# A four-layer kernel on one core: a quarter of the diagonal keys copied by GpSimd, loads and products put in another order, and two products given banks of their own

## The chip, the cores and the metric

The kernel runs on one core of one Trainium2 chip. The metric is the time of one execution in microseconds of the device; the numbers given are medians over runs on the same chip. The engines are called TensorE (PE in the rows), VectorE (DVE), ScalarE (ACT), GpSimd (POOL) and SyncE (SP); "ACTq" and "SPq" are the queues on which an engine issues transfers.

## The reference

The input x is (2, 2048, 512) in fp32. Four layers follow each other, each with a residual. B is the batch, N the tokens, F = 512 the features, H = 16 heads of D = 32.

```python
def modulated_linear(x, s, aff_w, aff_b, w, b):
    style = s @ aff_w.T + aff_b
    w_mod = w[None] * style[:, None, :]
    demod = rsqrt(sum(w_mod * w_mod, axis=2) + EPS)
    return einsum('bni,boi->bno', x, w_mod * demod[:, :, None]) + b

# layer 0: heads attend to each other within one token
kx = modulated_linear(x, s, k_...).reshape(B, N, H, D)
A = softmax(einsum('bnhd,bnjd->bnhj', kx, kx) / sqrt(D))
x = x + modulated_linear(einsum('bnhj,bnjd->bnhd', A, kx).reshape(B, N, F), s, o_...)
# layer 1: a weight of rank 30 for each batch, from a decoder
U = (mu @ W_dec + b_dec).reshape(B, 513, 30)
x = x + x @ (U @ V)[:, :-1] + (U @ V)[:, -1]
# layer 2: modulated linear, clipped
x = x + clip(einsum('blc,oc->blo', x * styles, weight) * dcoefs + bias)
# layer 3: several layer norms of x with gathered gains, three small MLPs,
# six weighted blocks concatenated, then W_int1, silu, W_int2, layer norm
h = ln(ln(x, pw_g[path], pw_b[path]), cp_g[comp], cp_b[comp]); t = ln(x, tm_g[..]); s = ln(x, ms_g[..])
x = x + mlp_ln(concat(w0*h, w1*t, w2*(x+m), w3*(x+n), w4*(x+r), w5*s), ...)
```

## The kernel before

The 4096 tokens are 32 tiles of 128 rows (T = 32), in groups of G = 4 tiles; the 512 features are C = 4 chunks of 128. A product that needs fp32 precision is made of three passes, from a high and a low part of either side (`x_hi`, `x_lo`, `w_high`, `w_low`). The order of work is written out by hand for every engine (`order`, `run_order`), each engine walks it by itself, and semaphores hold them together; so an instruction that waits holds up all that stands behind it on its engine.

**Layer 0** is the loop `attend(s)` for s = -1 to T+7, pipelined over the steps: step s works on several tiles at once. TensorE runs in each step: the transposes of v of tile s-2 (L686) and its scores (L693), the mix of tile s-3 with its weights (L650), the key projection of tile s (L676, 12 products of 512 columns), from s = 8 on the output projection of tile s-8 (L616, 12 products, into the bank `ps_o`), the mask of tile s-1 (L715), then the transposes of the mixed values `om` of tile s-3 (L738). The heads' products are small (32 x 32 blocks), and one operand is laid out as a block diagonal, 128 x 16 x 4 x 32: `k_diag` from the turned keys `kt`, and `at_diag` from the turned weights `at`. ScalarE writes both with four copies of 32 partitions each (`diagonal`, L1076). In a step the chain of a tile is: keys `kb` (VectorE L1427, GpSimd adds the bias, L1849), turned to `kt` (VectorE L1444), `k_diag` (ScalarE), scores, maximum and difference (L1392, L1396), exponential `e` (ScalarE L1103), its sum and inverse (L1416), the division (GpSimd L1843), turned to `at` (L1435), `at_diag` (ScalarE), mix (L650), turned back to `om` (L1403), scaled (GpSimd L1839), L738. GpSimd also scales the input `x_in` by the style (L1832), from which ScalarE and VectorE make the high and low parts for L676, and adds the output bias to the residual (L1826).

From tile 8 on (`SEED_AT`) the mask isn't a product: ScalarE writes it into the score bank beforehand (L1106). `prepare(s)` puts the side work in the steps: the small MLPs in 0 to 7 (their second results turned by `turn_rows(mlp_h2)`, L766, in step 6), the decoder's products L725 in the odd steps 5 to 19, the weights of layers 1 and 2 from step 20 on (`u_t`, the sum of the decoded U and its bias, at L1584 in step 22).

At the start SyncE issues the loads for the styles first (`cond`, `aff_k_t`, `aff_kbt`), then the first input; ScalarE's queue issues the four parts of W_k. TensorE runs six pieces of filling products (`keep_busy`) until the styles' loads have landed, then L89.

**Layers 1 to 3** are the loop `refine(s)`, with the layer-1 and layer-2 work a group of four tiles ahead: `lift(g)` makes `fh` and `fl` of the group's residual stream, `low_rank(g)` L940, `chunk(g, n)` the product of layer 2 (L616 into `ps_y`, evicted as `y` at L1226), and for each tile the layer-3 products: `x_product` (into `ps_3`, which takes the place of `ps_o`), then with t, s and h, silu to `g_out` (L1258), `turn_g`, the last product. GpSimd makes the gathered norms (`xn`, `h`, `tt`, `ss`: L1909 to L1933) and issues the gathers. The last steps of layer 0 overlap with the first of layer 1 (`order` above all from s = T+1 on). W_out's low part, `split("out")` on VectorE (L1631), is made in tile 0 of layer 3.

## Time and profile before

| | |
|---|---|
| runs (three) | 1000.88, 1000.90, 1002.64 us; median 1000.9 |
| the profiled execution | 1001.27 us, span 999.5 us |
| TensorE busy | 972.3 us of the span (97%) |
| GpSimd, VectorE, ScalarE busy | 693.6, 664.3, 501.4 us (69, 66, 50%) |
| the chain that ended last, by engine | PE 70%, POOL 9%, issue 8%, DVE 5%, DMA 3%, ACT 3% |

The span is cut into 40 slices of 25 us in the page; each digit is a busy share in tenths, for the TensorE clock it is what was granted, for DMA the mean busy share of the 16 DMA engines:

```
PE   8989999999999899999999999999999999999995
POOL 5656667575775449787777777778768768777861
PEclk8999999999999999999999999999999999999998
DMA  9644664464422562343133243332332233122220
```

Times are to be read from the start of the span. A row of a timeline gives start, duration, engine, line, operation, output and inputs with shape, and in brackets how long the engine was idle ahead of it and what ended that.

### The profile page before, as it was taken

What the parts mean: (1) busy time and instruction counts of PE and PEld (TensorE: products, weight loads), DVE (VectorE), ACT (ScalarE), POOL (GpSimd) and SP (SyncE); (2) the same over time, 40 slices, a digit from 0 to 9 for tenths busy, and PEclk for the clock granted to TensorE, in tenths of its full rate; (3) what the DMA queues carried; (4) which work ended last, traced back from release to release, by engine and by line L of the source; (5) the groups of instructions that cost most, each with busy time, mean ns of one, the idle gap of its engine ahead of it and who ended that gap; (6) DMA issues with size and microseconds to landing.
All of it is one profiled execution on the core that took longest, in us unless ns stands there. A gap on an engine that the chain in (4) does not pass through costs nothing.

```text
span 999.5 us, 18149 instructions
## 1 busy us (share of the span) xinstructions
PE 972.3 (97%) x6540; PEld 775.5 (78%) x6540; DVE 664.3 (66%) x1215; ACT 501.4 (50%) x792; POOL 693.6 (69%) x634
## 2 busy tenths in 40 slices
PE   8989999999999899999999999999999999999995
PEld 5667777777787677888888888888888888888884
DVE  6688767688878778666665658566567556664542
ACT  2888878787887544343342443334234324323332
POOL 5656667575775449787777777778768768777861
PEclk8999999999999999999999999999999999999998
DMA  9644664464422562343133243332332233122220
GB/s 291 223 144 126 218 225 150 161 218 139 152 90 81 185 213 87 109 121 119 66 109 106 93 130 100 118 110 66 101 116 90 80 101 126 67 91 108 79 76 23
DMA packets 58558, 125.11 MB, mean 125 GB/s; under 512 B 8052, under 2 KB 12534, under 8 KB 57445
## 3 DMA queue, kind: packets, MB, share of 16 engines
q1 hardware_dynamic: 46116, 80.95, 24.2%
q0 software_dynamic: 11776, 41.95, 13.4%
q8 instruction: 53, 0.87, 0.3%
q10 hardware_dynamic: 576, 1.05, 0.3%
q14 instruction: 37, 0.30, 0.1%
HBM read 105.98 MB, written 17.95 MB: 124 GB/s over the span
## 4 chain that ended last, share of the span: by engine, by line
PE 70%; POOL 9%; issue 8%; DVE 5%; DMA 3%; ACT 3%; SPq 1%; POOLq 0%; DVEq 0%; ACTq 0%
PE ps L609 34%; PE ps_k L676 7%; PE ps_y L616 6%; PE ps_o L616 5%; PE tp L621 4%; PE ps_v L650 2%; PE ps_s L693 2%; DMA xb<-in_x_wide 1%; PE ps_u L725 1%; PE ps_z L940 1%; POOL h L1909 1%; PE tp L952 1%; DMA id_rows<-in_id_rows 1%; PE ps_vt L686 1%; PE ps_t L738 1%
## 5 line engine op out<-in xcount | busy, mean ns | idle before, releaser
L1895 POOL TENSOR_TENSOR rstd<-var_eps,half 128x1 f32<-128x1 f32 x95 | 53.6, 565 | 101.5 <-DVE var_eps L1649 100.7
L1258 ACT ACTIVATE g_out<-ps 128x512 f32<-128x512 f32 x32 | 19.1, 597 | 167.2 <-PE ps L1057 167.2
L1839 POOL TENSOR_TENSOR om<-om,bc 128x512 f32<-128x512 f32 x32 | 41.4, 1292 | 65.1 <-DVE om L1403 65.0
L1076 ACT ACTIVATE at_diag<-at 32x512 f32<-32x512 f32 x128 | 80.3, 628 | 9.2 <-DVE at L1435 7.6
L1655 DVE TENSOR_SCALAR shift_n<-mean_var,rstd 128x1 f32<-128x1 f32 x96 | 20.5, 214 | 96.6 <-POOL rstd L1895 94.2
L1076 ACT ACTIVATE k_diag<-kt 32x512 f32<-32x512 f32 x128 | 80.2, 626 | 1.1
L1826 POOL TENSOR_SCALAR xb<-xb,bias_o 128x512 f32<-128x512 f32 x32 | 52.9, 1653 | 39.9 <-DMA xb<-in_x_wide 39.8
L1212 ACT ACTIVATE h<-h,shift_n,rstd 128x512 f32<-128x512 f32 x32 | 26.1, 816 | 84.7 <-DVE shift_n L1655 84.7
L1635 DVE TENSOR_TENSOR t_lo<-tp,t_hi 128x512 fp32r<-128x512 f32 x64 | 43.8, 684 | 29.8 <-ACT t_hi L1208 29.8
L676 PE MATMUL ps_k<-wk_hi,xh 128*128 128x512 f32 x128 | 54.1, 426 | 0.5 <-DVE xl L1451 0.5
L1955 POOL DMA_INDIRECT path_rows<-in_path,pid x32 | 39.5, 1235 | 19.5 <-POOL pid L1943 19.5
L609 PE MATMUL ps<-wx_high,x_hi 128*128 128x512 f32 x128 | 53.0, 414 | 0.0
L609 PE MATMUL ps<-wt_high,t_hi 128*128 128x512 f32 x128 | 52.7, 412 | 0.0
L616 PE MATMUL ps_o<-oh,wo_hi 128*128 128x512 f32 x128 | 50.3, 393 | 0.5 <-DVE xb L1383 0.5
L1928 POOL TENSOR_TENSOR o<-f,x3s 128x512 f32<-128x512 f32 x31 | 50.4, 1625 | 0.6 <-DMA out<-o 0.4
L609 PE MATMUL ps<-wx_high,x_lo 128*128 128x512 f32 x128 | 50.4, 393 | 0.0
L1917 POOL TENSOR_TENSOR tt<-xn,comp_rows 128x512 f32<-128x512 f32 x32 | 50.2, 1569 | 0.0
L609 PE MATMUL ps<-wt_high,t_lo 128*128 128x512 f32 x128 | 50.1, 392 | 0.0
L609 PE MATMUL ps<-wt_low,t_hi 128*128 128x512 f32 x128 | 50.0, 391 | 0.0
L609 PE MATMUL ps<-wx_low,x_hi 128*128 128x512 f32 x128 | 50.0, 390 | 0.0
L616 PE MATMUL ps_o<-ol,wo_hi 128*128 128x512 f32 x128 | 50.0, 390 | 0.0
L676 PE MATMUL ps_k<-wk_lo,xh 128*128 128x512 f32 x128 | 49.9, 394 | 0.0
(317 smaller groups left out, 3193.9 us busy)
## 6 DMA issues: line engine op xcount, KB each, us to landing
raw<-in_dec_w SPq DMA_DIRECT2D x30, 512.0 KB, 5.8
...
```

What stands on the lines that cost most here:

```text
L609: mm = nc.tensor.matmul(out_ps[:, :], x[:, c, :], w_[:, c, :], start=first and n == 0, stop=last and n == len(terms) - 1)
L616: mm = nc.tensor.matmul(out_ps[:, :], w_[:, c, at_], x[:, c], start=n == 0, stop=n == len(terms) - 1)
L621: mm = nc.tensor.transpose(bank[:, c, :], src[:, c * P:(c + 1) * P], ident[:, :])
L676: mm = nc.tensor.matmul(ps_k[:, :], x[:, c, :], w_[:, c, :], start=first and n == 0, stop=last and n == len(some) - 1)
L1076: last = nc.scalar.activation(dst[g, :, q, :], src[g, :, :], ACT.Copy)
L1635: nc.vector.tensor_tensor(lo[n][:, :, :], bank[:, :, :], hi[n][:, :, :].bitcast(F32), ALU.subtract).then_inc(lo_ready[n], 1)
L1826: nc.gpsimd.tensor_scalar(xb[n % 3][:, :], xb[n % 3][:, :], bias_o[:, fo:fo + 1], None, ALU.add).then_inc(xb_ready, 1)
L1839: nc.gpsimd.tensor_tensor(om[:, :], om[:, :], bc[:, STYLE_O, t // TB, :], ALU.mult).then_inc(mix_step, 1)
L1895: nc.gpsimd.tensor_tensor(rstd[:, k:k + 1], var_eps[:, k:k + 1], half[:, :], ALU.pow).then_inc(norm_step[k], 1)
L1917: nc.gpsimd.tensor_tensor(tt[:, :], xn[:, :], comp[:, F:2 * F], ALU.mult).then_inc(t_ready, 1)
L1928: nc.gpsimd.tensor_tensor(o[:, :], f2[:, :], x3s[f % 4][:, :], ALU.add).then_inc(o_ready, 1)
L1955: nc.gpsimd.indirect_dma_start(dst[:, :], None, I[table], bass.IndirectOffsetOnAxis(pid[:, k:k + 1], 0)).then_inc(landed, 16)
```

## The change

- **Start.** The loads of `cond` and `aff_kbt` go from SyncE's queue to the head of ScalarE's, ahead of W_k; `keep_busy` runs four pieces in place of six.
- **Diagonal keys.** In the steps 2 to 8 (`SHARED`) ScalarE copies three quarters of `k_diag`; GpSimd copies the fourth (`last_quarter`), as the first instruction of its step, ahead of `x_in`'s scaling. TensorE's scores wait for it through `xm_ready`, whose values `x_count` counts on.
- **Mask.** The last tile's mask is a product again (`seeded`).
- **`lift(0)`** on ScalarE (1 instruction, `fh`) goes from ahead of step T+1 to within it, behind `e` and `w_high`, ahead of `at_diag`.
- **Banks.** The output product of tile 31 goes to `ps_t`'s bank (`o_bank`) and waits for `ol` of the last tile in place of the residual of tile 30; `x_product(0)`, which writes where `ps_o` was, now waits for the residual of tile 31 (`x1_ready`, T). The fourth chunk's product of layer 2 goes to `tp[1]` (`y_bank`) and waits for the last mix alone; the first turn of `tt` then waits for that chunk's eviction.
- **W_out's low part** goes on VectorE from tile 0 to tile 1, ahead of that tile's `g_lo` and `s_lo`, with the ends of layers 1 and 2 behind these. Tile 0's silu is kept in a buffer of `x3s` (`g_rows`), so that it waits for stores of layer 0 and not for that.
- **Small ones.** `u_t`'s sum goes from VectorE to GpSimd (step 22); `turn_rows(mlp_h2)` goes from step 6 to step 7.

The core of the diff:

```diff
     for s in range(-1, T + 1):
         yield "attend", s
-    if engine == "ACT":
-        yield "lift", 0
     yield "attend", T + 1
...
+    SHARED = range(2, 9)
...
+        def seeded(t):
+            return SEED_AT <= t < T - 1
+        def g_rows(d):
+            return x3s[3][:, :] if d == 0 else g_out[:, :]
+        def x_count(t):
+            return t + 1 + len([s for s in SHARED if s < t])
...
+        def o_bank(n):
+            return ps_o[:, :] if n < T - 1 else ps_t[:, :, :].rearrange("p c q -> p (c q)")
+        def y_bank(n):
+            return tp[1][:, :, :].rearrange("p c q -> p (c q)") if n == C - 1 else ps_y[:, :]
...
@@ SyncE
-            sp.dma_start(cond[:, :, :], I["cond_t"].rearrange("(c p) b -> p c b", p=P)).then_inc(style_k_in, 16)
-            sp.dma_start(aff_kbt[:, :, :], I["aff_bt"]).then_inc(style_k_in, 16)
@@ TensorE
-            keep_busy(ps_o, 6)
+            keep_busy(ps_o, 4)
...
                 pe.wait_ge(ol_ready, G * (g + 1))
-                if later(n, 1):
+                if n == T - 1:
+                    pe.wait_ge(ol_ready, T)
+                elif later(n, 1):
                     pe.wait_ge(x1_ready, n)
...
                     pe.wait_ge(k_diag_ready, t + 1)
-                    if t >= SEED_AT:
+                    if t + 1 in SHARED:
+                        pe.wait_ge(xm_ready, x_count(t + 1) + 1)
+                    if seeded(t):
...
-                if has(1) and s - 1 < SEED_AT:
+                if has(1) and not seeded(s - 1):
...
-                if s == 6:
+                if s == 7:
                     pe.wait_ge(mlp_step, 14)
                     pe.wait_ge(table_ready, 3)
                     turn_rows(mlp_h2, ps_rows_t).then_inc(rows_turned, 1)
-                if s == 7:
...
-                if later(n, 1):
+                if n == C - 1:
+                    pe.wait_ge(v_ready, T)
+                elif later(n, 1):
                     pe.wait_ge(y_ready, n)
...
                     pe.wait_ge(w_lo_ready, 1)
-                    pe.wait_ge(ol_ready, T)
+                    pe.wait_ge(x1_ready, T)
                 product(ps_3, "x3", Wt["x"], last=False).then_inc(l3x_done, 1)
...
-                        pe.wait_ge(v_ready, T)
+                        pe.wait_ge(y_ready, C)
                     turn(tt, tp[1]).then_inc(turned["t"], 1)
@@ ScalarE
+            act.dma_start(cond[:, :, :], I["cond_t"].rearrange("(c p) b -> p c b", p=P)).then_inc(style_k_in, 16)
+            act.dma_start(aff_kbt[:, :, :], I["aff_bt"]).then_inc(style_k_in, 16)
...
-            def diagonal(dst, src):
-                for q in range(Q):
+            def diagonal(dst, src, count=Q):
+                for q in range(count):
...
-                    if SEED_AT <= t + 1 < T:
+                    if seeded(t + 1):
...
-                    diagonal(k_diag[p], kt[p]).then_inc(k_diag_ready, 1)
+                    diagonal(k_diag[p], kt[p], Q - 1 if s in SHARED else Q).then_inc(k_diag_ready, 1)
...
+                if s == T + 1:
+                    lift(0)
@@ VectorE
                 if s == 22:
-                    dve.wait_ge(u_back, 16 * B)
-                    nc.vector.tensor_tensor(u_t[:, :], u_got[0:B * LOW, :], tab_part[0:B * LOW, :], ALU.add).then_inc(u_step, 1)
...
+                if b == 3:
+                    dve.wait_ge(turned["g"], 1)
...
-                if ahead and k >= 1:
+                if c == 1:
+                    split("out")
+                elif ahead and k >= 1:
                     if s != 0:
                         layer1_end(g, k - 1)
                     layer2_end(g, k - 1)
...
                     low("s", c, tp[1])
+                if c == 1:
+                    layer1_end(g, k - 1)
+                    layer2_end(g, k - 1)
                 if c == 0:
                     split("h")
                     low("h", 0, tp[0])
                     hot(0)
-                    split("out")
                     x3_low(1)
@@ GpSimd
+            def last_quarter(s):
+                t, p, last = s - 1, (s + 1) % 2, slice(D * (Q - 1), D * Q)
...
+                pool.wait_ge(k_step, nth(KEYS, "turned", t + 1))
+                if later(t, 2):
+                    pool.wait_ge(scores_done, t - 1)
...
+                nc.gpsimd.tensor_copy(k_diag[p][last, :, Q - 1, :], kt[p][last, :, :]).then_inc(xm_ready, 1)
+                pool.wait_ge(xm_ready, x_count(s) + 1)
             def attend(s, has):
+                if s in SHARED:
+                    last_quarter(s)
...
+                if s == 22:
+                    pool.wait_ge(u_back, 16 * B)
+                    nc.gpsimd.tensor_tensor(u_t[:, :], u_got[0:B * LOW, :], tab_part[0:B * LOW, :], ALU.add).then_inc(u_step, 1)
```

GpSimd in the steps 2 and 3 of layer 0 (`wo_sq` and `mlp_rstd` are side work), before:

```order
L1860 TENSOR_TENSOR wo_sq<-wo_raw 128x512 x2
L1832 TENSOR_TENSOR x_in<-x_in,style_t 128x512
L1843 TENSOR_TENSOR e<-e,rinv 128x512
L1849 TENSOR_TENSOR kb<-kb,bias_k 128x512
L1860 TENSOR_TENSOR wo_sq<-wo_raw 128x512 x2
L1863 TENSOR_TENSOR mlp_rstd<-mlp_var,half 96x1
L1832 TENSOR_TENSOR x_in<-x_in,style_t 128x512
L1839 TENSOR_TENSOR om<-om,bc 128x512
L1843 TENSOR_TENSOR e<-e,rinv 128x512
L1849 TENSOR_TENSOR kb<-kb,bias_k 128x512
```

and with the change:

```order
L1914 TENSOR_TENSOR wo_sq<-wo_raw 128x512 x2
L1870 COPY k_diag<-kt 32x16x32
L1886 TENSOR_TENSOR x_in<-x_in,style_t 128x512
L1897 TENSOR_TENSOR e<-e,rinv 128x512
L1903 TENSOR_TENSOR kb<-kb,bias_k 128x512
L1914 TENSOR_TENSOR wo_sq<-wo_raw 128x512 x2
L1917 TENSOR_TENSOR mlp_rstd<-mlp_var,half 96x1
L1870 COPY k_diag<-kt 32x16x32
L1886 TENSOR_TENSOR x_in<-x_in,style_t 128x512
L1893 TENSOR_TENSOR om<-om,bc 128x512
L1897 TENSOR_TENSOR e<-e,rinv 128x512
L1903 TENSOR_TENSOR kb<-kb,bias_k 128x512
```

One copy (L1870) stands at the head of each of the two steps, ahead of `x_in` and all that follows on this engine.

ScalarE in the last steps of layer 0, from `e` of tile 30 on, before (`a_buf` is a piece of layer 2's weight, `fh` the high part of the residual stream for layers 1 and 2):

```order
L1106 ACTIVATE ps_s<-mask_rows 128x512
L1076 ACTIVATE k_diag<-kt 32x16x32 x4
L1124 ACTIVATE w_high<-a_buf 128x512
L1076 ACTIVATE at_diag<-at 32x16x32 x4
L1235 ACTIVATE fh<-xt 128x2048
L1087 ACTIVATE oh<-ps_t 128x4x128
L1097 ACTIVATE v<-ps_vt 128x512
L1103 ACTIVATE e<-low 128x512
L1124 ACTIVATE w_high<-a_buf 128x512
L1076 ACTIVATE at_diag<-at 32x16x32 x4
```

and with the change:

```order
L1100 ACTIVATE k_diag<-kt 32x16x32 x4
L1148 ACTIVATE w_high<-a_buf 128x512
L1100 ACTIVATE at_diag<-at 32x16x32 x4
L1111 ACTIVATE oh<-ps_t 128x4x128
L1121 ACTIVATE v<-ps_vt 128x512
L1127 ACTIVATE e<-low 128x512
L1148 ACTIVATE w_high<-a_buf 128x512
L1261 ACTIVATE fh<-xt 128x2048
L1100 ACTIVATE at_diag<-at 32x16x32 x4
```

The mask's copy into `ps_s` is gone, and `fh` stands four instructions further back, straight ahead of the last `at_diag` (tile 31's), behind `e` and `w_high`.

VectorE at the end of tile 0 of layer 3 and in tile 1, before (`h`, `tp` are the norm's inputs, the suffixes `_lo` the low parts for the products):

```order
L1721 TENSOR_SCALAR one_hot<-id_rows,codes 128x128
L1631 TENSOR_TENSOR wout_low<-out_raw,wout_high 128x2048
L1697 TENSOR_TENSOR x_lo<-xt,x_hi 128x512
L1641 BN_STATS stats<-h 128x6
L1645 BN_AGGR mean_var<-stats 128x2
L1649 TENSOR_SCALAR var_eps<-mean_var 128x1
L1655 TENSOR_SCALAR shift_n<-mean_var,rstd 128x1
L1641 BN_STATS stats<-tp 128x6
L1645 BN_AGGR mean_var<-stats 128x2
L1649 TENSOR_SCALAR var_eps<-mean_var 128x1
```

and with the change:

```order
L1671 BN_AGGR mean_var<-stats 128x2
L1675 TENSOR_SCALAR var_eps<-mean_var 128x1
L1681 TENSOR_SCALAR shift_n<-mean_var,rstd 128x1
L1667 BN_STATS stats<-tp 128x6
L1671 BN_AGGR mean_var<-stats 128x2
L1675 TENSOR_SCALAR var_eps<-mean_var 128x1
L1661 TENSOR_TENSOR t_lo<-tp,t_hi 128x512
L1742 TENSOR_TENSOR x3s<-tp,shift 128x512
L1681 TENSOR_SCALAR shift_n<-mean_var,rstd 128x1
L1657 TENSOR_TENSOR wout_low<-out_raw,wout_high 128x2048
L1661 TENSOR_TENSOR g_lo<-tp,g_hi 128x512
L1661 TENSOR_TENSOR s_lo<-tp,s_hi 128x512
```

The piece begins two rows later, behind `x_lo`'s and the statistics' first rows. `wout_low` stands ten rows further back than before, behind a shift of tile 1, with `g_lo` and `s_lo` behind it.

## Rows read from the trace of the kernel before

**Rows 1.** Waits of PE: engine, line, waited for, total us, times, longest us
```profile
PE ps_v L650 <- ACT at_diag L1076: 4.3, 5, 1.9
...
PE ps_t L738 <- DVE ol L1373: 1.2, 2, 0.7
...
PE tp L621 <- issue: 0.9, 1, 0.9
...
PE tp L621 <- POOL tt L1917: 0.9, 1, 0.9
...
PE ps_y L616 <- ACT y L1226: 0.6, 1, 0.6
...
PE ps_o L616 <- DVE xb L1383: 0.5, 1, 0.5
```

**Rows 2.** Engine time by stretch: busy us (count) per engine, PEclk, DMA share, GB/s
```profile
76.00:77.00 1.00, 1.00 (x6) 1.00 (x7) 1.00 (x2) 0.98 (x2) 0.00 (x0) 0.52 0.00 0
...
88.87:246.00 157.13, 156.17 (x1653) 116.97 (x1657) 119.37 (x193) 126.98 (x214) 106.05 (x84) 1.00 0.51 176
...
400.60:999.50 598.90, 587.37 (x2881) 489.08 (x2879) 355.49 (x711) 209.66 (x323) 437.95 (x420) 1.00 0.30 96
```

**Rows 3.** Timeline, start: start us, duration us, engine line operation [idle before <-releaser]
```profile
7.22 3.09 PE L89 MATMUL ps_x<-cond,wsq 128*128 128x2 f32 x16 [1.63 <-DMA aff_kbt<-in_aff_bt]
...
34.29 1.04 POOL L1832 TENSOR_TENSOR x_in<-x_in,style_t 128x512 f32<-128x512 f32 x1 [2.92 <-DMA x_in<-in_x_turned]
...
35.98 1.05 POOL L1843 TENSOR_TENSOR e<-e,rinv 128x512 f32<-128x512 f32 x1 [0.65 <-DVE rinv L1416]
```

**Rows 4.** Timeline, three durations that bound the GpSimd copy's price
```profile
0.87 0.53 POOL L1813 MEMSET mask_rr<- 128x512 f32 x1
...
71.52 2.54 ACT L1076 ACTIVATE k_diag<-kt 32x512 f32<-32x512 f32 x4
...
360.58 3.37 POOL L1826 TENSOR_SCALAR xb<-xb,bias_o 128x512 f32<-128x512 f32 x1 [5.84 <-DMA xb<-in_x_wide]
```

**Rows 5.** Timeline, steps 3 and 4
```profile
45.20 1.30 POOL L1839 TENSOR_TENSOR om<-om,bc 128x512 f32<-128x512 f32 x1 [0.40 <-DVE om L1403]
...
58.88 1.90 PE L650 MATMUL ps_v<-at_diag,v 128*32 128x128 f32 x32 [1.86 <-ACT at_diag L1076]
```

**Rows 6.** Timeline, steps 6 to 8
```profile
74.73 2.55 ACT L1076 ACTIVATE at_diag<-at 32x512 f32<-32x512 f32 x4
...
75.99 0.88 PE L766 MATMUL ps_o<-ident,xb 96*128 96x96 f32 x4 [2.01 <-DVE xb L1497]
...
77.65 1.94 PE L693 MATMUL ps_s<-k_diag,kt 128*32 128x128 f32 x32
...
77.88 1.66 POOL L1870 TENSOR_TENSOR demod_t<-vareps_ko,half_ko 128x8 f32<-128x8 f32 x1 [2.50 <-DVE vareps_ko L1549]
...
81.78 1.29 POOL L1839 TENSOR_TENSOR om<-om,bc 128x512 f32<-128x512 f32 x1 [1.22 <-DVE om L1403]
...
88.80 0.50 PE L676 MATMUL ps_k<-wk_hi,xh 128*128 128x512 f32 x1
```

**Rows 7.** Timeline, step 22 and the steps of the last tiles
```profile
237.02 0.68 DVE L1584 TENSOR_TENSOR u_t<-u_got,tab_part 64x512 f32<-64x512 f32 x1
...
331.53 1.91 ACT L1235 ACTIVATE fh<-xt 128x2048 fp32r<-128x2048 f32 x1
...
331.91 0.69 DVE L1396 TENSOR_TENSOR low<-ps_s,mx 128x512 f32<-128x512 f32 x1
...
373.82 0.74 DVE L1383 SCALAR_TENSOR_TENSOR xb<-ps_o,demod_t,xb 128x512 f32<-128x512 f32 x1
...
373.98 0.48 PE L609 MATMUL ps<-wx_high,x_hi 128*128 128x512 f32 x1
```

**Rows 8.** Timeline, layers 1 to 3, tiles 0 and 1
```profile
390.25 2.28 DVE L1631 TENSOR_TENSOR wout_low<-out_raw,wout_high 128x2048 fp32r<-128x2048 f32 x1
...
390.32 3.35 POOL L1911 TENSOR_TENSOR h<-h,path_rows 128x512 f32<-128x512 f32 x1
```

32 lines of the change are left out of this document (23 added, 9 removed).

## The prediction

> **What bounds the kernel now.** I read the busy times first: TensorE is busy 972.3 of 999.5 us, so all that any rearrangement can win is its 27.2 us of idle time and what it runs at a lowered clock. The engine time by stretch says where that is [rows 2]: from 88.9 to 246 us TensorE is busy 156.17 of 157.13, at full clock, and from 400.6 us to the end 587.37 of 598.90. In these two stretches it is the bound; a microsecond won ahead of one is carried to the end, and one lost as well. The waits of TensorE then name the places outside them: 4.3 us for the block-diagonal weights in five waits, 1.2 for `ol`, in tile 1 of layer 3 two of 0.9 [rows 1], 1.6 for the first loads [rows 3], and 2.0 for a small sum ahead of L766 [rows 6]. The change has an edit near each of these. So I follow three stretches: start to 88.8, the end of layer 0 to 374, and tiles 0 and 1 of layer 3 up to 400.
>
> **Start (loads, `keep_busy`).** L89 starts at 7.22, having waited 1.63 for `aff_kbt`, the third issue of SyncE's queue [rows 3]. At the head of another queue it lands earlier and two filling pieces fewer are in the way: 1.6 to 2.0 us earlier for the first styles and the first `x_in`. I count nothing of it at the end, because the next thing that is late is a transfer: the fourth tile's input is waited for by GpSimd until 34.29, after 2.92 us of idleness, and the bytes ahead of it are the same. Behind it GpSimd waits 0.65 more for the inverse sum [rows 3], which comes from the compute chain; at most that is won. Bounds: 0 and 0.65 us at step 2.
>
> **The fourth quarter on GpSimd (steps 2 to 8).** It saves ScalarE one of four copies, 2.54 / 4 = 0.63 us a step, and costs GpSimd one of 32 x 512. No row of before shows it. The nearest are GpSimd's 128 x 512 memset, 0.53, and its slowest one-input pass of that size, 3.37 [rows 4]. An ordinary pass with two inputs of that size, `e`, takes 1.05 [rows 3]. The copy reads one operand, so I put it between memset and `e` at 0.75, and keep 0.53 and 3.37 for the range.
> In step 3 the copy, then `x_in`, stand ahead of `om`, which had 0.40 of idle time [rows 5]: 0.75 - 0.40 = 0.35 late for `om`, `e` and `kb`, against 0.63 saved ahead of ScalarE's `at_diag`: TensorE's mix comes some 0.2 earlier. In step 4 the wait before the mix is 1.86 [rows 5], and its chain is `kb`, `at`, `at_diag`, in which `k_diag` has no part: `at_diag` starts when `at` is done, so that wait stays.
>
> **Steps 6 and 7 (`turn_rows` a step later, and the copy).** The wait of 2.01 ahead of L766 goes [rows 6]. In the microsecond behind it the granted clock is 0.52 [rows 2], the lower level of 1.2 GHz after TensorE had stood idle, and the 32 score products take 1.94 us [rows 6]. So there seems to be 2.0 plus about 1.3 of slowed products to win. Most of it isn't there: the mix of that step needs `at_diag`, which ScalarE ends at 74.73 + 2.55 = 77.28 [rows 6], so TensorE now waits there, and then GpSimd binds. From the end of `demod_t` (77.88 + 1.66 = 79.54) it had `x_in` 1.05, idle 1.22 waiting for `om`, `om` 1.29, `e` 1.05 [rows 6], then `kb`. With the change: 0.2 earlier, copy 0.75, and no idle: 0.2 + 1.22 - 0.75 = 0.67 earlier for `kb`, and so for the keys of step 8, which TensorE starts at 88.80 [rows 6] and from which on it is full. **I take 0.6 for all that lies ahead of 88.8**; with the clock lowered again at the new wait it is 0.3.
>
> **Step 22 (`u_t` on GpSimd).** VectorE spends 0.68 on it [rows 7], ahead of the maximum from which `ol` follows, for which TensorE waits 0.6 to 0.7 (one of two such waits [rows 1]). GpSimd idles at that point. Bounds 0 and 0.68; **0.4**, since the next operation that is late, `at_diag`, is not helped in full.
>
> **End of layer 0 (mask, `lift(0)`).** ScalarE's mask copy and `fh`, 1.91 us up to 333.44, stood ahead of two evictions and the `e` of tile 31, which started at 334.3. The difference it needs is ready at 331.91 + 0.69 = 332.60 [rows 7], so `e` starts some 1.6 earlier; of that GpSimd's and VectorE's order lets 1.05 through to `at` and `at_diag`. `fh` now stands ahead of `at_diag`, and fits in before `at` is done. Against three of TensorE's waits for `at_diag` and `ol` in this stretch: **1.0** at 344 us, bounds 0.5 and 1.6.
>
> **Banks.** They take away the waits for `y` (0.6) and for the residual (0.5) [rows 1]. But `x_product(0)` starts at 373.98 and from now on waits for the residual of tile 31, which VectorE made from 373.82 to 374.56, behind other work [rows 7]. TensorE arrives earlier, and waits there instead: **0** for TensorE, and 0.5 to 0.6 earlier for VectorE and GpSimd; bounds -0.6 and 1.1.
>
> **W_out's low part.** It takes 2.28 us of VectorE in tile 0, and a GpSimd pass that overlaps it takes 3.35 [rows 8] where one of the same shape takes 1.30 [rows 5]. `tt` comes 0.9 late from that, and 0.9 more is waited behind it [rows 1]. In tile 1 it stands ahead of `g_lo` and `s_lo`, which TensorE needs a group of 12 products later, and beside it GpSimd issues gathers. The two waits of 0.9 go, and some 0.2 come back: **1.6**, bounds 0.2 and 2.1.
> The Trainium skill ("SBUF — State Buffer", section "SBUF: two separate sides") says that VectorE and GpSimd share a port pair as an exclusive lock: a VectorE instruction with two SBUF inputs and a GpSimd instruction that reads SBUF block each other for their whole length. By that rule the 3.35 above is a pass that stood still, so trace and rule agree; but it also speaks against the copies: the fourth rival.
>
> **Sum.** 0.6 + 0.4 + 1.0 + 0 + 1.6 = 3.6 us. The profiled execution took 1001.27 us, its span 999.5; it becomes 997.7. The median of the runs is 0.4 lower than that execution, 1000.9, so I forecast **997.3 us**.
>
> **Rivals.**
> *The clock stays up early.* If TensorE's shorter idle times in the steps 5 to 7 don't bring the clock down, the products that ran at 0.52 [rows 2] take half the time, the chains that begin at them move too, and up to 2.6 us are won ahead of 88.8 in place of 0.6: 995.3. For it: the longest of the waits go or shrink. Against: GpSimd's order in step 7, as worked out.
> *The wait moves with W_out's part.* The 2.28 us [rows 8] now hold up `g_lo` and `s_lo`, TensorE waits for these in tile 1, and the late 1.6 is given back: 998.9. For it: nothing on VectorE got shorter. Against: the new place has 12 products of slack.
> *GpSimd becomes the bound, slower.* At the place where the copy stands ahead of `x_in`, `om`, `e` and `kb`, it must fit in 0.40 (step 3) and 1.22 (step 7) of slack, with the 0.6 that the early part wins: 2.2 us for two copies. At the contended price of 3.37 each [rows 4] they cost 6.74, so 4.5 are lost early, against 3.0 won late: 1.5 slower, 1002.4. It decides the sign from a copy of (2.2 + 3.0) / 2 = 2.6 us. Against it: only a GpSimd pass that ran beside one of VectorE's took that long.
> *The copies stand behind `xl`.* VectorE's `xl`, two inputs, follows straight on the `kt` that releases the copy. If the copy waits it out, it comes 0.68 later, the length of such a VectorE pass [rows 7], in both steps in which it counts, 3 and 7: 1.4 us worse, 998.7. For it: the pass of 3.35 beside `wout_low` [rows 8], the case that the Trainium skill's rule describes. Against it: the copy and `xl` are released at nearly the same moment, and step 7's copy stands behind `demod_t`, after `xl`.
> *The start gains nothing and the early edits don't meet the wait*: some 1000.0.
>
> **How the numbers follow.** About 2.0 us (0.2%) is what a measurement of this kernel can tell from no change: faster means under 998.9, slower over 1002.9. Main case 0.40, of which 0.39 lies under 998.9 and 0.01 within. Clock 0.22, faster. Moved wait 0.18, at the boundary: 0.09 faster, 0.09 same. Copies behind `xl` 0.10: 0.06 faster, 0.04 same. GpSimd bound 0.05: 0.01 same, 0.04 slower. The last 0.05: 0.04 same, 0.01 slower. Together faster 0.76, same 0.19, slower 0.05. The range: below, the clock case's 2.6 with the upper bounds 0.6, 1.6 and 2.1 of the others are 6.9, so 994.0, and I go to 993.8; above, the lower bounds 0, 0.5 and 0.2 with the early 0.6 lost in part leave 0.5: 1000.4.
>
> **What would show it.** Right: L89 near 5.5 us; the copies at 0.6 to 1.1 us; no wait ahead of L766 but one of 1.5 to 2 ahead of the mix in step 7; TensorE's key projection of step 8 at 88.2; no wait for `y` nor for the residual of tile 30, but one for that of tile 31; `h`'s pass at 1.3 in tile 1. Wrong: copies over 2 us, the wait in step 4 longer than 1.9, TensorE waiting for `g_lo` or `s_lo`, or a key projection of step 8 before 87 us.

## The result, and the profile after

| | before | with the change |
|---|---|---|
| median of 20 runs | 999.36 us (996.49 to 1002.84) | 1003.79 us (1000.2 to 1006.9, without one disturbed execution) |
| ratio, 95% interval | | 1.0037 [1.0027, 1.0048] |
| profiled execution, span | 1001.27, 999.5 us | 1003.55, 1001.8 us |
| TensorE busy | 972.3 us | 973.0 us |
| GpSimd, ScalarE busy | 693.6, 501.4 us | 702.1, 497.9 us |

The forecast was 997.3 us, 3.6 less than before, in a range of 993.8 to 1000.4. The kernel became 0.37% slower by the ratio, 3.7 us (the two medians lie 4.4 apart). TensorE does the same work and idles 28.8 us in place of 27.2; some of its work also ran at the lower rate.

Its waits with the change, in the view of [rows 1]:

```profile
PE ps_v L667 <- ACT at_diag L1100: 6.2, 6, 1.9
...
PE tp L638 <- DVE t_lo L1661: 3.5, 3, 2.9
...
PE ps_t L759 <- DVE ol L1402: 1.6, 2, 1.2
...
PE ps L626 <- DVE xb L1412: 1.5, 1, 1.5
...
PE ps_x L654 <- DVE wk_sq L1395: 0.7, 1, 0.7
...
PE ps_t L759 <- POOL om L1893: 0.8, 2, 0.5
```

The wait for the block-diagonal weights has grown from 4.3 to 6.2 us, and three waits are new: 2.9 for `t_lo` in one place, 1.5 for a residual, 0.7 for W_k's squares. The two waits of 0.9 in tile 1, that for `y`, that for the residual of tile 30 and that ahead of `turn_rows` are gone, as forecast. So nearly every wait that the change aimed at has gone, and others stand in their place.

To see where, one can lay marks on TensorE's timeline and take the time between two of them. This also keeps apart what varies from one execution to the next: single executions of the kernel before lie 6 us apart, and much of the spread that the traces show arises ahead of the first mark. The marks are the first products on `u_row` in step 2, the mixes (L650) of tiles 6, 20, 21 and 31, `x_product(0)`, and the products with the table (`one_hot`) that close tiles 0, 1 and 2 of layer 3. From the timelines, in us; "before, again" is a second execution of the kernel before (run b2), told of below:

```
                              before   before, again   the change
span start to u_row            35.05          34.84        37.14
u_row to mix of tile 6         61.44          59.86        59.76
mix of tile 20 to 21           11.23          11.24        11.81
mix of tile 21 to 31           94.58          94.54        93.72
mix of 31 to x_product(0)      33.53          33.52        33.64
table product 0 to 1           18.82          18.79        16.77
table product 1 to 2           22.04          22.02        26.49
```

**Start.** The styles' products begin earlier, as meant, and what follows is late. With the change:

```profile
5.76 3.57 PE L89 MATMUL ps_x<-cond,wsq 128*128 128x2 f32 x16 [0.80 <-DMA aff_kbt<-in_aff_bt]
...
11.98 1.93 PE L654 MATMUL ps_x<-wk_sq,sq_wide 128*32 128x512 f32 x8 [0.73 <-DVE wk_sq L1395]
...
17.43 1.91 PE L695 MATMUL ps_k<-wk_lo,xh 128*128 128x512 f32 x4
...
10.62 0.63 ACT L1086 ACTIVATE wk_hi<-wk_raw 128x512 fp32r<-128x512 f32 x1 [0.78 <-DMA wk_raw<-in_w_k_t]
```

and before:

```profile
16.20 1.09 PE L676 MATMUL ps_k<-wk_lo,xh 128*128 128x512 f32 x4
...
8.47 0.63 ACT L1064 ACTIVATE wk_hi<-wk_raw 128x512 fp32r<-128x512 f32 x1 [0.82 <-DMA wk_raw<-in_w_k_t]
```

L89 is 1.46 us earlier (7.22, [rows 3]). But the last of W_k's four parts, now behind two small loads, is ready for ScalarE at 10.62 and not at 8.47. TensorE waits for its squares, and its four products of a first-tile term, 1.09 us before, take 1.91: half the rate. The key projection of step 8, forecast for 88.2, starts at 89.22 (88.80 before).

**Copies.** With the change, GpSimd's copies in the steps 2 and 3 and TensorE's waits ahead of the mixes of tiles 1, 2, 4 and 5:

```profile
33.32 0.96 POOL L1870 COPY k_diag<-kt 32x512 f32<-32x512 f32 x1
...
46.28 0.61 POOL L1870 COPY k_diag<-kt 32x512 f32<-32x512 f32 x1
...
53.66 1.08 PE L667 MATMUL ps_v<-at_diag,v 128*32 128x128 f32 x32 [0.76 <-ACT at_diag L1100]
...
61.71 1.08 PE L667 MATMUL ps_v<-at_diag,v 128*32 128x128 f32 x32 [1.87 <-ACT at_diag L1100]
...
78.56 1.08 PE L667 MATMUL ps_v<-at_diag,v 128*32 128x128 f32 x32 [1.91 <-ACT at_diag L1100]
...
88.21 1.08 PE L667 MATMUL ps_v<-at_diag,v 128*32 128x128 f32 x32 [0.70 <-ACT at_diag L1100]
```

The seven copies take 0.96, 0.61, 0.93, 0.99, 0.93, 0.61 and 0.98 us, all between the ends of 0.53 and 3.37. In the two steps that the sum priced, 3 and 7, it is 0.61, and with the gaps around it the copy makes `x_in` 0.8 later (against the kernel without copies, run ns): that price, 0.75, was right. The other five begin while VectorE's `xl` runs; each of them ends 0.48 us after `xl`, as in step 5:

```profile
61.24 0.64 DVE L1480 TENSOR_TENSOR xl<-x_in,xh 128x512 fp32r<-128x512 f32 x1
...
61.37 0.99 POOL L1870 COPY k_diag<-kt 32x512 f32<-32x512 f32 x1 [1.57 <-DVE kt L1473]
```

That is the mechanism of the fourth rival, but not in the steps 3 and 7, where no `xl` runs beside the copy. What went wrong is in step 3, on ScalarE, before and with the change:

```profile
48.28 2.55 ACT L1076 ACTIVATE at_diag<-at 32x512 f32<-32x512 f32 x4
...
51.05 2.55 ACT L1100 ACTIVATE at_diag<-at 32x512 f32<-32x512 f32 x4 [0.99 <-DVE at L1464]
```

Before, ScalarE came to `at_diag` just as `at` was done. With the change ScalarE is free earlier and waits 0.99 us, because `at` is late by the copy: its relief wins nothing there. The wait of 1.86 in step 4 [rows 5] has stayed; the wait of 2.01 ahead of L766 [rows 6] has become 1.91 ahead of the mix of tile 4; and 0.70 ahead of tile 5's is new.

**Step 22.** `u_t`'s sum on GpSimd, and the wait for `ol`:

```profile
232.49 1.26 POOL L1939 TENSOR_TENSOR u_t<-u_got,tab_part 64x512 f32<-64x512 f32 x1
...
243.09 0.63 PE L759 MATMUL ps_t<-ident,om 128*128 128x128 f32 x4 [1.25 <-DVE ol L1402]
```

It takes 1.26 us there (0.68 on VectorE, [rows 7]), ahead of the residual's bias, which VectorE waits for; the wait of 0.7 [rows 1] has become 1.25.

**Banks.** TensorE's wait ahead of `x_product(0)`, and VectorE's residual of tile 31 that ends it:

```profile
374.28 0.47 PE L626 MATMUL ps<-wx_high,x_hi 128*128 128x512 f32 x1 [1.46 <-DVE xb L1412]
...
373.38 0.75 DVE L1412 SCALAR_TENSOR_TENSOR xb<-ps_t,demod_t,xb 128x512 f32<-128x512 f32 x1
```

The start is 374.28, 373.98 before [rows 7]. (One thing told ahead of the prediction is to be corrected: `ps_3` stands where `ps_t` was, not where `ps_o` was. That is why `x_product(0)` has to wait for tile 31 once its product is in `ps_t`.)

**W_out's low part.** Tiles 0 and 1 of layer 3, and then TensorE in tile 2:

```profile
390.61 1.29 POOL L1968 TENSOR_TENSOR h<-h,path_rows 128x512 f32<-128x512 f32 x1
...
397.34 2.28 DVE L1657 TENSOR_TENSOR wout_low<-out_raw,wout_high 128x2048 fp32r<-128x2048 f32 x1
...
397.60 2.95 POOL L2012 DMA_INDIRECT path_rows<-in_path,pid  x1 [0.28 <-POOL pid L2000]
...
420.20 1.09 PE L638 MATMUL tp<-ident,ss 128*128 128x128 f32 x4 [2.95 <-DVE t_lo L1661]
...
421.08 1.06 PE L638 MATMUL tp<-ident,h 128*128 128x128 f32 x4
```

GpSimd's pass L1968 takes 1.29 and not 3.35 [rows 8]: that step was right, and tile 1 is 2.05 us shorter. But the part, 2.28 us long, now begins 0.26 ahead of the first gather for tile 2. That gather's issue takes 2.95 us and ends at 400.55, 0.93 after the part has ended. GpSimd's norms of tile 2 come late, then `t_lo`; TensorE, ahead by 2, waits 2.95 for it, and its transposes then take 1.09 for the 0.60 that they take elsewhere. The granted clock there:

```profile
420.00:422.00 2.00, 1.80 (x9) 1.83 (x10) 1.65 (x3) 2.00 (x4) 1.92 (x3) 0.50 0.00 0
```

is 0.50, the lower level, 1.2 GHz. Tile 2 loses 4.45 us.

### The profile page after: what moved, and what is told of

It reads as the page before. It is cut to its first block, busy times and chain, and to the rows that moved or that the text cites. A ratio compares the mean times of both kernels' runs of the same rounds, so it can differ in the third digit from the quotient of the medians.

```text
span 1001.8 us, 18164 instructions
## 1 busy us (share of the span) xinstructions
PE 973.0 (97%) x6537; PEld 776.1 (77%) x6537; DVE 664.9 (66%) x1214; ACT 497.9 (50%) x784; POOL 702.1 (70%) x642
## 4 chain that ended last, share of the span: by engine, by line
PE 72%; POOL 10%; issue 7%; DVE 5%; DMA 3%; ACT 2%; SPq 0%; ACTq 0%; POOLq 0%; DVEq 0%
PE ps L626 36%; PE ps_k L695 7%; PE ps_y L633 7%; PE ps_o L633 5%; PE tp L638 5%; PE ps_v L667 2%; PE ps_s L714 2%; DMA xb<-in_x_wide 1%; PE ps_u L746 1%; PE tp L974 1%; PE ps_z L962 1%; PE ps_t L759 1%; POOL h L1966 1%; PE ps_vt L705 1%; POOL om L1893 1%
## 5 line engine op out<-in xcount | busy, mean ns | idle before, releaser
L1100 ACT ACTIVATE k_diag<-kt 32x512 f32<-32x512 f32 x121 | 75.9, 627 | 1.1
L2012 POOL DMA_INDIRECT path_rows<-in_path,pid x32 | 41.8, 1305 | 19.7 <-POOL pid L2000 19.7
L1985 POOL TENSOR_TENSOR o<-f,x3s 128x512 f32<-128x512 f32 x31 | 52.5, 1694 | 0.2
L695 PE MATMUL ps_k<-wk_hi,xl 128*128 128x512 f32 x128 | 50.1, 396 | 0.0
L626 PE MATMUL ps<-ws_high,s_hi 128*128 128x512 f32 x128 | 49.8, 389 | 0.0
```

The lines of the kernel that those rows point to most:

```text
L626: mm = nc.tensor.matmul(out_ps[:, :], x[:, c, :], w_[:, c, :], start=first and n == 0, stop=last and n == len(terms) - 1)
L695: mm = nc.tensor.matmul(ps_k[:, :], x[:, c, :], w_[:, c, :], start=first and n == 0, stop=last and n == len(some) - 1)
L1100: last = nc.scalar.activation(dst[g, :, q, :], src[g, :, :], ACT.Copy)
L1985: nc.gpsimd.tensor_tensor(o[:, :], f2[:, :], x3s[f % 4][:, :], ALU.add).then_inc(o_ready, 1)
L2012: nc.gpsimd.indirect_dma_start(dst[:, :], None, I[table], bass.IndirectOffsetOnAxis(pid[:, k:k + 1], 0)).then_inc(landed, 16)
```

## The experiments

Each run has its median and, behind it, its ratio to the kernel before, measured beside it on the same chip, with a 95% interval. The ratios hold the whole; the marks, from one trace of each run, hold the parts.

### w0: W_out's low part back in tile 0

```diff
-                if c == 1:
-                    split("out")
-                elif ahead and k >= 1:
+                if ahead and k >= 1:
...
                     hot(0)
+                    split("out")
                     x3_low(1)
```

> The changed kernel with W_out's low part back in tile 0 of layer 3, all else as changed. Theory (the wait moved to the gathers): with the part in tile 1 the first gather of tile 2 is issued in 2.95 us instead of 1.05, its results come late, TensorE waits 2.95 us for t_lo in tile 2 and runs its next products at the lower rate, 4.45 us in all, after a gain of 2.04 in tile 1. Undone, the distance from x_product(0) to the table product of tile 2 (62.0 us with the change, 59.6 before) is 59.0 to 60.0, and the time is 2.4 us below the changed kernel's. Rival (the 2.9 us wait is an accident of that one execution): the distance is that of the changed kernel less nothing systematic, and the time rises by the 2.04 of tile 1.

Measured: 1001.74 us, 1.0021 [1.0005, 1.0038], by the ratios 1.6 below the change (2.4 expected; the intervals overlap). The gather, and TensorE's waits:

```profile
400.55 1.05 POOL L2008 DMA_INDIRECT path_rows<-in_path,pid  x1 [0.28 <-POOL pid L1996]
...
PE tp L638 <- DVE t_lo L1661: 1.3, 3, 0.6
...
PE tp L638 <- POOL tt L1970: 0.9, 1, 0.9
...
PE tp L638 <- issue: 0.9, 1, 0.9
```

The gather takes 1.05 again, the two waits of 0.9 are back, the wait for `t_lo` is 0.6. From `x_product(0)` to table product 2: 60.4 us, 62.0 with the change, 59.6 before; 59.0 to 60.0 was expected. The part was in tile 1 in six executions with its own subtraction: the gather took 2.94 or 2.95 in all of them, the stretch from table product 0 to 1 16.8 us in all six, and from 1 to 2 24.0 to 27.9, 26.0 on average. With the part in tile 0, ten other kernels and executions give 18.8 and 22.0 to 22.2, w0 22.8. So the move wins 2.0 and loses 3.9 on average.

The long gather is no accident; what follows from it varies. In two of the six (ns and t6) the granted clock stays at 1.00, and TensorE waits 1.8 and 2.1 us:

```profile
416.38 0.63 PE L638 MATMUL tp<-ident,ss 128*128 128x128 f32 x4 [1.81 <-DVE t_lo L1661]
```

From `x_product(0)` to table product 2 these two take 59.6 and 59.8 us, as before. In the other four the wait is 2.4 to 3.0 us, the granted clock falls to 0.50 behind it, and the stretch takes 61.8 to 63.4. So the gather gives back the 2.0 that were won, and the longer wait with the fallen clock makes the loss. Why the first norm behind the gathers starts up to 1.2 us later in one execution than in another, these runs don't show.

### k6: six filling pieces

```diff
-            keep_busy(ps_o, 4)
+            keep_busy(ps_o, 6)
```

> The changed kernel with six filling pieces at the start in place of four. Theory (clock): with four pieces TensorE stands idle from 4.96 us, and its products then run at the lower rate until 20.5 us (before: until 14); six pieces bring the full rate back by 14 us, the products of the first tile (16.8 to 20.5 us) take 1.8 us less and the first mix starts at 43 us or below in place of 44.79; time 1 to 2 us below the changed kernel's. Rival (order of the loads: W_k's parts come 0.9 us later behind the two small ones, and the squares wait for them): six pieces change nothing or cost 0.5, the first mix stays at 44.8.

Measured: 1003.39 us, 1.0048 [1.003, 1.0066], no better than the change where 1 to 2 us were expected; first mix at 43.63, the full rate by 16. The wait for the squares was 3.5 us. One execution against another said that the pieces help by 1.2 us, the medians that they don't. That was left for the runs below.

### ns: no copies on GpSimd

```diff
-    SHARED = range(2, 9)
+    SHARED = range(0)
```

> The changed kernel with all four quarters of the diagonal keys on ScalarE again. Theory (GpSimd binds): a copy takes 0.96 us and stands ahead of x_in, om, e and kb; the mixes of tiles 1 and 5 start 0.7 and 1.2 us late for it; without it the key projection of step 8 comes 1.0 to 1.5 us earlier against the first mix, and the time is 1 us below the changed kernel's. Rival (ScalarE binds, the copies help): at_diag comes 0.63 later in steps 2 to 8 and the time rises by 0.6 or more.

Measured: 1001.24 us, 1.0017 [1.0004, 1.003]. From u_row to the mix of tile 6: 58.28 us, 59.76 with the change, and no wait ahead of tile 5's mix. The time is 2.0 us below the change's by the ratios. Over the six executions that have all seven copies this stretch takes 59.4 to 61.2 us, 60.3 on average, without the one with the earlier `turn_rows`; over six without any 58.3 to 59.9, 58.7 on average: a difference of 1.6 us.

The time between single mixes says more, for from the mix of tile 1 on it repeats within 0.06 us where the clock doesn't fall. With a copy in step 3 the mixes of tiles 0 and 1 lie 8.5 to 8.9 us apart, without it 8.2 (8.4 in boa4, and 9.0 in two runs that wait for an input). From the mix of tile 3 to that of tile 6 it is 26.4 with the copies of the steps 7 and 8 and 25.6 without. So the copies cost 0.3 to 0.7 in step 3 and 0.8 in step 7, 1.1 to 1.5 us. The rest of the 1.6 is a fallen clock in step 4, which makes the time between the mixes of tiles 2 and 3 10.4 us in place of 8.8. It fell in four of the eight traces with a copy in step 3 (k6, ks, t6, c37) and in one of the ten without (the first of the kernel before): more often with the copy, but too few to decide.

### ud: `u_t` back on VectorE

```diff
+                    nc.vector.tensor_tensor(u_t[:, :], u_got[0:B * LOW, :], tab_part[0:B * LOW, :], ALU.add).then_inc(u_step, 1)
...
-                    nc.gpsimd.tensor_tensor(u_t[:, :], u_got[0:B * LOW, :], tab_part[0:B * LOW, :], ALU.add).then_inc(u_step, 1)
```

> The changed kernel with the sum for u_t back on VectorE. Theory: on GpSimd it takes 1.26 us ahead of the residual's bias, VectorE's residual waits for that, and TensorE's wait for ol in step 22 grew from 0.67 to 1.25; undone it is 0.7 again and the time 0.6 lower. Rival: the wait has another cause (the stretch begins 0.4 later anyway); it stays at 1.2.

Measured: 1003.51 us, 1.0036 [1.0019, 1.0054], which can't tell 0.6 us. The marks can: from the mix of tile 20 to 21 it is 11.21, with the change 11.81. All seven traces with the sum on GpSimd have 11.76 to 11.82, all eleven with it on VectorE 11.19 to 11.25. It costs 0.6.

### ks: the start undone

```diff
+            sp.dma_start(cond[:, :, :], I["cond_t"].rearrange("(c p) b -> p c b", p=P)).then_inc(style_k_in, 16)
             sp.dma_start(affs[0], I["aff_k_t"].rearrange("(c p) f -> p c f", p=P)).then_inc(style_k_in, 16)
+            sp.dma_start(aff_kbt[:, :, :], I["aff_bt"]).then_inc(style_k_in, 16)
...
-            keep_busy(ps_o, 4)
+            keep_busy(ps_o, 6)
...
-            act.dma_start(cond[:, :, :], I["cond_t"].rearrange("(c p) b -> p c b", p=P)).then_inc(style_k_in, 16)
-            act.dma_start(aff_kbt[:, :, :], I["aff_bt"]).then_inc(style_k_in, 16)
```

> The changed kernel with its start undone (cond and aff_kbt on SyncE's queue again, six filling pieces). Theory (W_k's parts behind two small loads): the wait ahead of the products of squares goes from 0.7 to 3.9 us to none or under 0.5, TensorE is at the full rate by 15 us, the first mix starts at 42.5 to 43.5 us instead of 43.5 to 46.2; time 1.5 below the changed kernel's. Rival (the first mix is set by the transfer of the fourth tile's input and by the copy in step 2): it stays above 44.5.

Measured: 1000.82 us, 1.0012 [0.9998, 1.0027]; a wait of 0.2 for the squares, first mix at 41.44, earlier than expected. It is 2.5 us better than the change.

### t6: `turn_rows` in step 6

```diff
-                if s == 7:
+                if s == 6:
                     pe.wait_ge(mlp_step, 14)
                     pe.wait_ge(table_ready, 3)
                     turn_rows(mlp_h2, ps_rows_t).then_inc(rows_turned, 1)
+                if s == 7:
```

> The changed kernel with turn_rows in step 6 again. Theory (a wait there is 2.0 us, but another one takes its place): TensorE waits 1.5 to 2.0 ahead of it and no longer 1.9 ahead of the mix of tile 4; the mix starts 1.0 to 2.0 us later and what is left at the mix of tile 6 is 0.5 to 1.5 later than with the change. Rival (GpSimd's order in step 7 binds alone): the mix of tile 6 comes at the same distance from the first mix, 52.1 us.

Measured: 1002.15 us, 1.0024 [1.0008, 1.0039], and in the trace:

```profile
75.98 0.81 PE L787 MATMUL ps_o<-ident,xb 96*128 96x96 f32 x4 [2.00 <-DVE xb L1527]
```

The wait is there again, 2.00, and that ahead of tile 4's mix is gone. From u_row to the mix of tile 6: 61.81, against 60.3 on average with the later place; but the clock fell in step 4 here, which is 1.6 us. From the mix of tile 3 to that of tile 6 it is 27.20, and 26.39 with the change: the later place wins 0.8 beside the copies. Without copies it wins 1.6 (27.2 in both executions of the kernel before, 25.6 in ns). So the two edits don't add: with the early `turn_rows` the copy in step 7 costs nothing (27.20 with and without it), with the late one 0.8. The ratio doesn't bear the 0.8 out: t6 lies 1.3 us under the change where it should lie above it. The intervals overlap, and that stays open.

### b2: the kernel before, again

> The kernel before once more, unchanged, for its profile: how far the first 40 us vary from one execution to the next. If the first mix starts within 0.5 us of 42.7 the start's 2.1 us of the changed kernel is its own; if it starts over 44 it is chance.

Measured: 999.34 us (one execution), first mix at 42.48, within the 0.5. In the steps up to 8 this execution was 1.6 us faster than the first, since the clock did not fall in step 4. That is as much as several terms of my sum.

### best1: four parts undone

The edits of w0, ns, ud and ks together.

> The changed kernel with four of its parts undone: the loads and the filling pieces as before, no copies on GpSimd, W_out's low part in tile 0, the sum for u_t on VectorE. Left are the later turn_rows, the last tile's mask and lift(0), and the banks. Theory (the kept parts are sound, the four are what cost): to x_product(0) the kernel takes 370.5 to 372.0 us of the span (before 374.0), tiles 0 to 2 as before, time 2 to 3.5 us below the kernel before. Rival (the kept parts win nothing either, the start varies by more than they do): within 1 us of the kernel before.

Measured: 997.14 us, 0.9973 [0.9962, 0.9983]: faster than the kernel before. `x_product(0)` at 370.88, table products as before. The later `turn_rows` and the pair of the last tile's mask and `lift(0)` are sound together; no run takes the mask and `lift(0)` apart. `x_product(0)` still waits 1.5 us for the residual.

### sh, c37: copies in some of the steps

On best1, `SHARED = range(4, 7)` and `SHARED = (3, 7, 8)`.

> The fastest version so far (the changed kernel with the start, the copies, W_out's part and u_t undone) with copies on GpSimd in the steps 4 to 6 alone. Theory (a copy costs only where GpSimd's chain x_in, om, e, kb is the late one, steps 3, 7 and 8): from the products on u_row in step 2 to the mix of tile 6 it stays at 58.3 us, plus or minus 0.3. Rival A (any copy costs its 0.96 us or a part): 59 or more. Rival B (ScalarE's relief helps in step 4, where TensorE waits 1.9 us for at_diag): 57.7 or less.

Measured: 995.58 us, 0.9963 [0.9951, 0.9976]; u_row to the mix of tile 6: 58.28, the same as best1's 58.27.

> The fastest version so far with copies on GpSimd in the steps 3, 7 and 8 alone. Theory: this carries the whole cost of the seven copies, 1.5 to 2.7 us: the same stretch takes 59.7 us or more where no lowered clock hits it, with a wait of 0.75 ahead of the mix of tile 1 and 0.7 ahead of that of tile 5. Rival (the cost is spread over all copies): 58.9 or less.

Measured: 998.34 us, 0.9989 [0.9977, 1.0002]; 61.00 us, and the two waits:

```profile
51.06 1.08 PE L669 MATMUL ps_v<-at_diag,v 128*32 128x128 f32 x32 [0.75 <-ACT at_diag L1100]
...
87.18 1.08 PE L669 MATMUL ps_v<-at_diag,v 128*32 128x128 f32 x32 [0.71 <-ACT at_diag L1100]
```

Part of the 61.0 is a lowered clock in step 4 (0.50 granted from 60 to 62 us), 1.6 us. Without it 59.4 would be left, between the theory's 59.7 and the rival's 58.9, and 1.1 over best1. So the copies in the steps 3, 7 and 8 carry the cost of 1.1 that all seven have at the least; in the steps 4 to 6 they neither cost nor win, though TensorE waits 1.9 us for ScalarE's `at_diag` there. The relief of ScalarE lies ahead of a wait for `at`, as the prediction had it.

### bo: tile 31's product in its old bank

```diff
-            return ps_o[:, :] if n < T - 1 else ps_t[:, :, :].rearrange("p c q -> p (c q)")
+            return ps_o[:, :]
...
-                if n == T - 1:
-                    pe.wait_ge(ol_ready, T)
-                elif later(n, 1):
+                if later(n, 1):
...
-                    pe.wait_ge(x1_ready, T)
+                    pe.wait_ge(ol_ready, T)
```

on best1.

> The fastest version so far with tile 31's output product in its old bank (the fourth chunk of layer 2 keeps its own). Theory (own bank for tile 31 only moves the wait): TensorE waits 0.5 for the residual of tile 30 and no longer 1.5 for that of tile 31; x_product(0) starts 0.5 to 1.0 us earlier against the last mix (33.6 us with the bank) and the time falls by as much. Rival (x_lo is ready no earlier): 33.6 stays within 0.2.

Measured: 995.88 us, 0.9966 [0.9953, 0.9979]. The wait of 1.5 is gone, and in its place:

```profile
PE ps_o L635 <- DVE xb L1410: 0.5, 1, 0.5
```

From the mix of tile 31 to `x_product(0)`: 32.87, and 32.64 to 32.92 in all five executions of this form, 33.4 to 33.7 in the others. Of the two new banks, that of tile 31 cost 0.8 us, and that of the fourth chunk wins about 0.7. The ratios can't tell this: 0.9966 here, 0.9973 for best1 and 0.9963 for sh, which both have the new bank.

### w1: a plain copy in place of W_out's low part

It leaves out the subtraction; the copy has one input.

```diff
+                    if n == "out":
+                        nc.vector.tensor_copy(flat(w_lo), flat(staged_raw[n])).then_inc(w_lo_ready, 1)
```

> The changed kernel with W_out's low part replaced by a plain copy of W_out at the same place of tile 1: the subtraction is left out, so the last product has a wrong low part. Theory (a VectorE pass that reads two operands in the on-chip buffer holds up GpSimd, a gather's issue too): with one operand the first gather of tile 2 is issued in 1.05 us instead of 2.95, GpSimd's norms of tile 2 start 1.9 earlier, TensorE's wait for t_lo in tile 2 falls from 2.95 to about 1. Rival (the gather waits for something else there, or the plain copy holds it up as well): it stays at 2.9.

Measured: 999.59 us, 0.9998 [0.9984, 1.0011]:

```profile
393.69 1.22 DVE L1658 CAST wout_low<-out_raw 128x2048 fp32r<-128x2048 f32 x1
...
393.95 1.88 POOL L2015 DMA_INDIRECT path_rows<-in_path,pid  x1 [0.28 <-POOL pid L2003]
...
414.11 0.63 PE L638 MATMUL tp<-ident,ss 128*128 128x128 f32 x4 [0.49 <-DVE t_lo L1664]
```

The theory was wrong in its reason. The copy, with one operand, takes 1.22 us and holds up the gather just as well: the issue ends at 395.83, 0.92 after the copy, as it ended 0.93 after the subtraction. It is shorter only because VectorE's pass is. The consequence stood: with a gather 1.07 us shorter TensorE waits 0.5 in tile 2, not 2.95, and table product 2 comes 58.2 us after `x_product(0)` in place of 62.0.

The Trainium skill ("SBUF — State Buffer", section "SBUF: two separate sides") tells this of a copy: while VectorE runs an instruction in a 2-port mode, which an fp32 copy triggers, GpSimd is locked out of the shared ports and can't write the descriptors of its transfers. The trace agrees for the copy, 1.22 us: the gather ends 0.92 behind it. For the subtraction, 2.28 us, the trace shows the same, 0.93 behind it.

### bol4, boa6, boa4: queue and filling pieces apart

On bo: four pieces with SyncE's queue; six with ScalarE's; four with ScalarE's.

> The fastest version (bo) with four filling pieces, the loads on SyncE's queue. Theory (the queue is the cause): as bo, the products on u_row at 34.4 us plus or minus 1, the time within 0.8 us of bo's 0.9966 of the kernel before. Rival (the pieces are the cause): u_row at 35.5 or later, TensorE at the lower rate until 20 us, 1 to 2 us slower.

> bo with cond and aff_kbt at the head of ScalarE's queue and six filling pieces. Theory (queue): 1 to 2 us slower than bo, the ratio to the kernel before 0.998, u_row at 35.5 to 37. Rival (pieces): as bo.

> bo with the whole start of the change: the two loads on ScalarE's queue and four pieces. Both theories: 1.5 to 2.5 us slower than bo; if it is within 0.8 us of bo, the start costs nothing and the difference between the changed kernel and the one with its start undone was chance.

| | queue of the two loads | pieces | ratio to before | u_row at |
|---|---|---|---|---|
| bo | SyncE | 6 | 0.9966 [0.9953, 0.9979] | 32.94 |
| bol4 | SyncE | 4 | 0.9979 [0.9968, 0.9991] | 34.62 |
| boa6 | ScalarE | 6 | 0.9997 [0.9983, 1.001] | 35.68 |
| boa4 | ScalarE | 4 | 0.999 [0.9976, 1.0004] | 37.90 |

The queue costs 1.1 us with four pieces, where the intervals overlap, and 3.1 with six, 2.1 on average. The pieces show nothing clear: six are 1.3 better on SyncE's queue (so bol4 isn't within the 0.8 of bo that was expected), 0.7 worse on ScalarE's and 1.1 worse in k6, all with intervals that overlap. In nine traces with the loads on ScalarE's queue its last W_k part comes at 9.89 to 11.54 us, in nine with SyncE's at 7.88 to 8.87; the products on `u_row` at 36.4 and 34.3 on average. boa4 shows what follows, its engine time by stretch:

```profile
10.00:14.00 4.00, 1.73 (x8) 0.23 (x8) 3.35 (x6) 1.38 (x3) 1.57 (x2) 0.50 1.07 267
...
14.00:18.00 4.00, 4.00 (x17) 3.49 (x14) 0.56 (x3) 0.60 (x1) 0.44 (x1) 0.50 1.06 279
...
18.00:20.00 2.00, 2.00 (x6) 1.52 (x6) 1.26 (x5) 0.00 (x0) 2.00 (x3) 0.50 1.08 360
```

```profile
PE ps_x L654 <- DVE wk_sq L1393: 3.2, 1, 3.2
```

and bol4's:

```profile
10.00:14.00 4.00, 4.00 (x14) 1.50 (x13) 3.52 (x6) 1.23 (x2) 1.30 (x1) 0.50 1.07 254
...
14.00:18.00 4.00, 3.87 (x20) 2.98 (x20) 1.16 (x6) 0.00 (x0) 2.16 (x3) 0.92 1.07 324
...
18.00:20.00 2.00, 2.00 (x5) 0.49 (x6) 1.53 (x4) 1.10 (x2) 0.86 (x1) 1.00 1.07 376
```

TensorE is idle for 3.2 us up to 12.27, waiting for W_k's squares, and is granted 0.50 until about 22 us; bol4, busy from 8 on, is at 0.92 from 14 to 18 and at the full clock behind it.

### shbo: sh and bo together

> bo with copies on GpSimd in the steps 4 to 6. If the relief of ScalarE in these steps is worth something the ratio is 0.9955 or less; if the copies there are neutral, as the stretch of 58.3 us in both says, it is bo's 0.9966 within the interval.

Measured: 996.32 us, 0.9971 [0.9961, 0.9981], as bo. The copies in the steps 4 to 6 are worth nothing. Between bo, sh and shbo no ratio decides; bo has the fewest parts and is the version to keep.

## Why the prediction was wrong, point by point

The terms, in us won, as forecast and as the marks give them (averages over the executions named above):

| step | forecast | measured |
|---|---|---|
| start: two loads, filling pieces | 0 | -2.1 |
| copies and `turn_rows`, up to step 8 | +0.6 | +0.3 (-1.3 and +1.6) |
| `u_t` on GpSimd | +0.4 | -0.6 |
| mask and `lift(0)` | +1.0 | +0.9 |
| banks | 0 | -0.1 (+0.7 and -0.8) |
| W_out's low part | +1.6 | -1.9 |
| sum | +3.6 | -3.5 |

For the copies and `turn_rows` the stretch from u_row to the mix of tile 6 is taken without the falls of the clock (1.6 us each where it fell in step 4, 0.7 in w0): 59.6 on average with both edits (59.4 to 59.8), 59.9 before.

- **Start: wrong, by leaving out what the step displaces.** The prediction counted how much earlier the styles come and called the rest hidden behind the fourth tile's input. It never asked what stands behind the two loads on ScalarE's queue: W_k's four parts, and behind the last of them TensorE's squares. They came 2.4 us later on average, more than the two issues, 0.48 and 0.51 us; where the rest comes from the runs don't show. That the fourth tile's input swallows what is won is half true: with the earliest start, bo's, 0.9 us were lost again between the first mix and the second, and there GpSimd waits 4.6 us for that input.
- **Copies: right on GpSimd, wrong for TensorE in step 3.** The price of 0.75 was right (0.8), and so was step 7: from `demod_t` to `kb` it is 5.66 us and 6.34 before, 0.68 earlier for the forecast 0.67. In step 3 the prediction set ScalarE's saving of 0.63 against a delay of 0.35 and had the mix 0.2 earlier. The two don't subtract: `at_diag` starts when the later of ScalarE and `at` is ready, and `at` was late. The mix came 0.3 to 0.7 later. That argument, "`at_diag` starts when `at` is done", the prediction made for step 4 and not for step 3.
- **The 2 us of wait ahead of L766: right** that it reappears ahead of the mix, 1.91.
- **`u_t`: wrong.** "GpSimd idles at that point" was read from 4.85 us of idleness ahead of `om`. The sum was put ahead of that gap, and between lie the residual's bias and `x_in`, for which VectorE waits. The lower bound of 0 was wrong for the same reason: an instruction that goes to another engine can cost there.
- **Mask, `lift(0)`: right**, 0.9 for 1.0.
- **Banks: right in the sum**, and in the place of the new wait.
- **W_out's low part: the step that failed most, 3.5 us of 7.1.** The gain in tile 1 was right, 2.0 for 1.6. What it would displace was named (the gathers beside it) and priced at 0.2, "some 0.2 come back". The row for its price was at hand, in the trace of before, and I did not use it:

```profile
382.57 1.08 POOL L1955 DMA_INDIRECT path_rows<-in_path,pid  x1 [0.28 <-POOL pid L1943]
...
382.81 2.35 DVE L1628 SCALAR_TENSOR_TENSOR ws_low<-raw,wv,ws_high 128x2048 fp32r<-128x2048 f32 x1
...
383.96 2.01 POOL L1955 DMA_INDIRECT comp_rows<-in_comp,pid  x1 [0.31 <-issue]
```

  `ws_low`, a pass like this one, runs from 382.81 to 385.16, and the gather that begins in it takes 2.01 us, 0.94 in the next tile. The gather that began 0.24 ahead of `ws_low` takes 1.08. So it matters which of the two starts first, and in tile 1 `wout_low` started 0.26 ahead. The second rival had the right form, the wait moves, and the wrong place: not `g_lo`, but the gathers, one tile further on. Its price, the gain given back, is what two of six executions show. In the others TensorE, 2 us ahead, ran into a chain that was later still (in the change's trace `t_lo` comes 1.2 us later than before, counted from `x_product(0)`), and its clock fell behind the wait.
- **The clock.** The prediction had it as a rival that wins 2.0, and in the main case as a loss of 0.3 at one wait. It cost more: at the start, where in four of nine executions with the loads on ScalarE's queue, and in none of nine with the other, the first tile's products took 1.91 for 1.09; and in tile 2. The four at the start all have four filling pieces (of seven that do); the two with six pieces waited as long for the squares, 3.3 and 3.5 us, without it. That the pieces have a part in it is not ruled out.
